# Keeping split weights in DRAM after the first of four blocks, in a one-core transformer layer in fp32

## What is computed

```python
x = x + attn(cond(x, cond_weights, itok_B_0_15), Wq, Wk, Wv, Wo, q_norm_w, k_norm_w)
x = x + ffn(cond2(x, weight, bias, lora_a, lora_b, scaling, itok_B_1_7), W_base, b_base, enc0, ...)

# cond:  einsum('bct,bcd->bdt', x, weights[condition])
# attn:  q = x @ Wq.T (32 heads), k = x @ Wk.T, v = x @ Wv.T (8 heads), rmsnorm(q), rmsnorm(k),
#        softmax(q k^T / sqrt(128) + alibi, causal) v, then @ Wo.T
# cond2: x @ weight.T + bias + a low-rank term chosen for each sequence
# ffn:   x @ W_base.T + b_base + 0.5 * (an inverse Fourier transform of masked low-rank terms)
```

## Time and profile before

| | us |
|---|---|
| median of 3 runs | 2668.3 |
| lowest and highest | 2659.5 and 2669.61 |
| the profiled execution | 2667.39 |
| its span, first to last instruction | 2665.6 |

### The profile page before, as it was taken

How to read it: one execution, slowest core, us unless ns; L and a number is a source line. 1 busy time by engine, 2 the same in 40 slices (tenths; PEclk the granted TensorE clock), 3 DMA queues, 4 the chain that set the end, 5 groups by cost and what they waited for, 6 DMA issues and landing times.

```text
span 2665.6 us, 32724 instructions
## 1 busy us (share of the span) xinstructions
PE 2441.8 (92%) x11676; PEld 1995.5 (75%) x11676; DVE 1811.7 (68%) x2830; ACT 1249.5 (47%) x2881; POOL 431.5 (16%) x336
## 2 busy tenths in 40 slices
PE   7989989898899999999899999898989989899988
PEld 5867767676678777777778777777768878787867
DVE  5557768676845767676854777767774686867682
ACT  3235545353524545454633555555542554545450
POOL 0101212120211111111121121112130121212021
PEclk8989999999999999999999999999999999999999
DMA  5261433525343141414234141423243132323241
GB/s 206 103 253 64 167 141 135 190 91 194 128 142 111 64 142 65 141 64 142 95 122 149 64 143 64 133 73 126 73 143 135 64 119 87 119 88 111 95 150 48
DMA packets 88436, 316.13 MB, mean 119 GB/s; under 512 B 12716, under 2 KB 13228, under 8 KB 87124
## 3 DMA queue, kind: packets, MB, share of 16 engines
q1 hardware_dynamic: 70292, 247.14, 27.4%
q10 hardware_dynamic: 10944, 37.54, 3.8%
q0 software_dynamic: 7040, 29.36, 3.0%
HBM read 282.54 MB, written 31.46 MB: 118 GB/s over the span
## 4 chain that ended last, share of the span: by engine, by line
PE 61%; DVE 21%; DMA 6%; issue 6%; ACT 4%; POOL 1%; ACTq 0%; POOLq 0%; DVEq 0%
PE main L926 50%; DVE ring L1367 9%; DMA raw<-in_wo 4%; PE qt_bank L1075 2%; ACT ring L1121 2%; DMA sums<-in_wo 2%; DVE qn L1501 2%; PE s_bank L1091 2%; DVE qn L1494 2%; DVE pt_lo L1557 1%; DVE score L1370 1%; PE pv_bank L1110 1%; PE s_bank L1092 1%; POOL rstd L1666 1%; DVE lefts L1367 1%
## 5 line engine op out<-in xcount | busy, mean ns | idle before, releaser
L926 PE MATMUL main<-ring,act_hi 128*128 128x512 f32 x3584 | 1155.8, 404 | 0.0
L926 PEld LDWEIGHTS main<-ring,act_hi 128*128 128x128 f32 x3584 | 646.4, 190 | 112.8
L926 PE MATMUL main<-ring,act_lo 128*128 128x512 f32 x1792 | 705.4, 394 | 0.0
L926 PE MATMUL main<-ring,lefts 128*128 128x512 f32 x2688 | 655.7, 403 | 45.4 <-ACT main L1121 24.6
L1367 DVE TENSOR_TENSOR ring<-raw,ring 128x1024 fp32r<-128x1024 f32 x448 | 607.1, 1364 | 89.5 <-ACT ring L1121 88.2
L1121 ACT ACTIVATE ring<-raw 128x1024 fp32r<-128x1024 f32 x448 | 473.4, 1061 | 400.7 <-PE main L926 274.4
L926 PEld LDWEIGHTS main<-ring,lefts 128*128 128x128 f32 x2688 | 517.8, 195 | 162.2 <-ACT main L1121 29.7
L1666 POOL TENSOR_TENSOR rstd<-mean,half 128x4 f32<-128x4 f32 (+1 forms) x192 | 179.7, 936 | 1606.8 <-DVE mean L1477 1606.8
L926 PEld LDWEIGHTS main<-ring,act_lo 128*128 128x128 f32 x1792 | 339.1, 189 | 75.4
L1075 PE MATMUL qt_bank<-ident,qn 128*128 128x128 f32 x640 | 108.5, 285 | 119.4 <-DVE qn L1501 62.8
L1243 ACT ACTIVATE sq<-main 128x128 f32<-128x128 f32 x640 | 168.8, 277 | 76.7 <-PE main L926 74.4
(11 more groups left out here) (142 smaller groups left out, 2595.3 us busy)
## 6 DMA issues: line engine op xcount, KB each, us to landing
raw<-in_wq SPq DMA_DIRECT2D x128, 512.0 KB, 4.1
raw<-t_scratch SPq DMA_DIRECT2D x128, 512.0 KB, 3.3
raw<-in_wo SPq DMA_DIRECT2D x96, 512.0 KB, 3.3
raw<-in_wkv SPq DMA_DIRECT2D x64, 512.0 KB, 4.2
sums<-in_wo ACTq DMA_DIRECT2D x32, 512.0 KB, 6.3
t_scratch<-sums ACTq DMA_DIRECT2D x32, 512.0 KB, 4.4
raw<-f_scratch SPq DMA_DIRECT2D x32, 512.0 KB, 4.0
acc<-in_x POOLq DMA_DIRECT2D x16, 512.0 KB, 3.6
```

The source lines that it names most:

```text
L926: mm = eng.matmul(bank, a, b, start=start and n == 0 and m == 0, stop=stop and n == len(terms) - 1 and m == 2, skip_group_check=further)
```

## The change

In block 0 each chunk is loaded and split as before, and then the two halves of 84 of the 112 chunks (all of `kv`, `q` and `f`, and the even ones of `o`; `is_kept`) are stored together, 1 MB, from `ring` to `w_scratch` in DRAM (`w_store`, issued by SP). In blocks 1 to 3 these chunks are loaded from there straight into their slot of `ring` (`ring{i}`, SP, 1 MB) with no work on ACT or DVE; the 28 odd chunks of `o` are loaded raw and split as before, and their raw load is issued just ahead of the 1 MB load of the chunk before. There are 4 raw buffers in place of 3 (the query gain takes the bytes of `score` to make room). Split chunks are planned at least 1.8 quarters apart in place of 1. `t_load` to `t_store` are spread out, with 5.5 quarters from load to `t1` in place of 3.5. `s1`, `s4` and `v7_add` go from POOL to DVE, at later places.

```diff
-RAWS = 3
+RAWS = 4
...
-LEFT_AT = (dict(s3=-9, s2=-3, s1=0.5, s4=2.5, op=(-8, -6, -2, 4.4, 8.4, 12.4, 16.4)),
+LEFT_AT = (dict(s3=-9, s2=-3, s1=2.6, s4=6.6, op=(-8, -6, -2, 4.4, 8.4, 12.4, 16.4)),
...
+def is_kept(kind, c):
+
+    return kind != "o" or c % 2 == 0
...
             if n >= SLOTS:
-                last = max(free[n - SLOTS] + AT["w_hi"], last + 1)
-            out.append(last)
+                if self.is_halves(n):
+                    before = max(free[n - SLOTS], before)
+                else:
+                    before = last = max(free[n - SLOTS] + AT["w_hi"], last + 1.8, before)
+            out.append(before)
         return out
+
+    def is_halves(self, n):
+
+        u, c = self.chunks[n]
+        kind, blk, number = self.units[u]
+        return blk > 0 and is_kept(kind, c)
...
-        self.load(n, ("w_lo", (n,)))
+        if self.is_halves(n):
+            if n + 1 < len(self.chunks) and not self.is_halves(n + 1):
+                self.load(n + 1, ("w_lo", (n + 1,)))
+            self.add(f"ring{n % SLOTS}", n)
+            return
+        if blk == 0:
+            self.load(n, ("w_lo", (n,)))
         self.add("w_hi", n)
+
+        def rest():
+            self.add("w_lo", n)
+            if blk == 0 and is_kept(kind, c):
+                self.add(f"w_store{n % SLOTS}", n)
...
-        for pair in range(KV_HEADS // 2):
-            self.right_factors(pair)
+
+        for at, pair in ((0, 0), (28, 1)):
+            self.right_factors(pair, at, 14)
+        for pair in (2, 3):
+            self.right_factors(pair, QUARTERS * (self.first_step["o", 0, pair - 2] + len(OPS)), 19)
...
         self.add("v7_out", k, tp)
-        self.add("v7_add", k, tp)
+        self.later(1.5, lambda: self.add("v7_add", k, tp))
...
+                elif stage.startswith("w_store"):
+                    n, = key
+                    w.wait_ge("w_lo", n)
+                    eng.dma_start(w_scratch[n], f32(ring[:, n % SLOTS, :, :])).then_inc(done[stage], 16)
+                elif stage.startswith("ring"):
+                    n, = key
+                    made = n % per_block
+                    w.wait_ge(f"w_store{made % SLOTS}", made)
+                    slot_free(w, n)
+                    eng.dma_start(f32(ring[:, n % SLOTS, :, :]), w_scratch[made]).then_inc(done[stage], 16)
```

More of the change, by code:

```diff
@@ L368, in prepare @@
             self.gather(blk)
-        self.load(n, ("w_lo", (n,)))
+        if self.is_halves(n):
[5 more added lines that the diff above has]
+            self.load(n, ("w_lo", (n,)))
         self.add("w_hi", n)
+        def rest():
+            self.add("w_lo", n)
+            if blk == 0 and is_kept(kind, c):
+                self.add(f"w_store{n % SLOTS}", n)
         if both:
-            self.add("w_lo", n)
+            rest()
         else:
-            self.later(AT["w_lo"] - AT["w_hi"], lambda: self.add("w_lo", n))
+            self.later(AT["w_lo"] - AT["w_hi"], rest)
     def blocks(self):
@@ L611 @@
 DMA_STAGES = ("coefs", "masks", "mixidx", "const", "mixw_load", "first", "raw", "x", "out", "f_store",
-              "t_load", "t_store", "fx_load", "fx_store")
+              "t_load", "t_store", "fx_load", "fx_store", "ring", "w_store")
 def is_dma(stage):
@@ L758, in setup_part, with slot_free @@
             return setup[:, UNIT_CHUNKS * slot + c, part, :]
+        per_block = len(order.chunks) // BLOCKS
+        w_scratch = nc.dram_tensor("w_scratch", [per_block, P, 2, CHUNK], F32).ap()
+        def slot_free(w, n):
+            before = n - SLOTS
+            if before < 0:
+                w.wait_ge("weff_mm", KT, n // UNIT_CHUNKS, n % UNIT_CHUNKS)
+                return
+            u, c = order.chunks[before]
+            unit = order.units[u]
+            if unit[0] == "o":
+                w.wait_ge("mm", order.first_step[unit] + c // 2, 2 + c % 2)
+            else:
+                w.wait_ge("mm", order.first_step[unit] + TILES - 1, c)
+            if unit[1] == 0 and is_kept(unit[0], c):
+                w.wait_ge(f"w_store{before % SLOTS}", before)
         def ring_part(n, part):
@@ L946, in weights_here @@
             def weights_here(n):
-                w.wait_ge("w_hi", n)
-                w.wait_ge("w_lo", n)
+                if order.is_halves(n):
+                    w.wait_ge(f"ring{n % SLOTS}", n)
+                else:
+                    w.wait_ge("w_hi", n)
+                    w.wait_ge("w_lo", n)
             for stage, key in order.stages:
@@ L1303, in _ @@
                     elif blk == 0:
+                        if pair > 0:
+                            w.wait_ge("mm", order.left_before[k], 3)
                         for i in range(4):
-                            w.wait_ge(f"t_store{i}", pair, 1)
+                            w.wait_ge(f"t_store{i}", min(pair + 1, 3), 1)
                     else:
```

81 lines of the change are left out of this document (36 added, 45 removed).

## The result

The changed kernel takes 2947.8 us (median of 4 runs, 2947.2 to 2953.5) against 2669.0 before: ratio 1.106, 95% interval 1.103 to 1.109. The profiled execution's span is 2945.5 us. I had forecast 2800, with a range up to 2930: the sign was right, the loss about twice the one forecast (+279 in place of +133).

The account below looks back on a forecast made before the run. PE was taken as the bound, with only its gaps and the slow stretches behind them to win. Block 0 +238 and blocks 1 to 3 -105 gave +133 on 2667.4, so 2800 us; 8-in-10 range 2650 to 2930.

Parts of the forecast that it names:

- the slow clock: Block 0: PE at its lower clock behind a dozen new waits of 3 to 5 us, +20 us, at most 30.
- Blocks 1 to 3, -105: Later blocks: 252 splits and POOL's sums go, so PE's waits and slow clock shrink; saves 105 us, bounds 80 and 120.
- Block 0, +238: First block: raw loads lose their lead, only one ahead where three were; 238 us longer, bounds +85 and +338.
- L: Block 0: time for a raw load right behind a 1 MB store to land, 5.1 us, bounds 3.3 and 6.1.
- The round, 7.9: Block 0, chunks in a row: store issue, load, upper half, lower half and hand-overs take 7.9 us per chunk (6.1 to 8.9).
- Unit ends: Block 0, eight ends other than around `o`: 26.3 us where 16.5 before; 9.8 us each, 78 in all (35 to 102).
- Around `o`: Block 0, four `o` units: 100.1 us from first upper half to query transposes, before 64.0; 36 each, 144 (65 to 188).
- End of the setup: Before block 0's first key transposes: five rounds put them at 184.8 instead of 167.86, costing 17 us (8 to 22).
- A store costs the next load nothing: Rival, chance 0.16: block 0 loads still land in 3.3 us, block 0 loses only 85, later blocks gain 120; 2632 us.
- Transfers as the bound in later blocks: Rival, chance 0.13: 1 MB loads land late, 57 us over later blocks, and block 0 is +314; 2933 us.
- Half of the store out of the way: Rival, chance 0.20: block 0 loads land in 4.2 us, rounds 7.0 and 8.5, +164 in block 0; 2726 us.
- Less saved: Rival, chance 0.07: other DVE work is as late in blocks 1 to 3, which save 60 in place of 105; 2845 us.

## Why the prediction was right and wrong, point by point

**The step that failed.** The mechanism of block 0 held. What failed is the size of one term of its sum, the slow clock: +20, at most +30, where PE's busy time rose by 104. A second term was too small as well, the length and number of the rounds, which left idle time at +279 where I had +218. The measured +279 is still inside what my upper bound leaves for idle time (338 less 30); the clock's 104 is what carried the time over the range.

**The bound.** Right. What changed the time was PE's gaps, and the slow matmuls behind them.

**Blocks 1 to 3, -105.** Right in sum: -99 by the stretches, -105 from block to block. The agreement to the microsecond is luck: my terms add up to 116, and I went on from the 120 that I had called "at most"; the waits for `lefts` were not in it; and with the sums left on POOL the same halves bring 74. It was wrong in what it rests on. I gave nearly all to splits that go away, and to POOL's operation 1.6 of the 2.8 us that I took off one wait for the gain. I had its row, a gain of 2.12 us that ends behind POOL's sum, and took it for one place; the group mean of the earlier trace rows, 1364 ns against 1.22 us undisturbed, said that there were more of them, 44 among the lower halves alone. Either half of the change alone gets some 70 of the 104 us. The query scaling went with the splits, as I had said; the gain went mostly with the sums. The new wait of 3 us for ring loads was 1.3, though they landed in 6.2 us and not in 5.8; the 4 us a block that I held back for dense places did not show as a wait for loads.

**Block 0, +238.** The mechanism is what I described: SP's queue at `w_lo`, the load behind the store, ACT's head of queue, 581 us of waits for `raw`. The size was +383, beyond my upper bound of +338. Below, unit ends, `o` units and the setup divide it by place, and the slow clock by kind: two ways to count the same microseconds, not to be added.

- *L.* Assumed 5.1; measured 5.7 for a lone load behind a store (page, `in_wq`), within the bounds. The single store in front costs 2.4 us over the 3.3 of the earlier trace rows; behind the load in place of in front of it, it costs 0.9 (4.2).
- *The round, 7.9.* 8.4 at best, 9.4 on average in the row of four that is shown. What is over comes from the term that I had as a sentence and not as a number: ACT stands at `w_hi`, the query's lower half on DVE gets late by it, and the next `w_lo` stands behind that.
- *Unit ends.* I gave 26.3 us from the first upper half to the scores; here it is 31.3 (264.30 to 295.62, the first row below), and at the same unit end before it was 16.8. At the unit end of the earlier trace rows, 16.5 us before, it is 33.4. From the first `o` row's start to the second's it is 231.9 us (364.14 to 596.07) in place of 146.7, of which the `o` row takes 53 (next point), so two unit ends take 32: 16 us each, not 9.8. With the two next points taken off the 386 us of block 0, 145 are left for all of them, not 78.
- *Around `o`.* 100.1 forecast from the first upper half to the query transposes, 117.1 measured, by the last two rows below; before 64.0. The four cost 53, 53, 46 and, where the two `f` units follow, 70 us: 222, not the 147 of my `o` and `f` terms.
- *End of the setup.* 17 forecast; the key transposes start at 186.63, 18.8 us later than before. Right.
- *Slow clock.* The step that failed most. I added 20 us; PE's busy time rose by 104. The measured times of the two places above hold their share of it, which my rounds, made of loads and halves alone, did not: in place of the dozen new waits that I counted there are 58 gaps where there were 20, and many are longer than 5 us. So of the 145 us missed in block 0, 84 are slow matmuls and 61 idle time (279 against 218).

In the changed kernel: PE's first score behind the row of four; then ACT's first and last upper half of the first `o` row, and PE's transposes behind it.

```profile
295.62 0.44 PE L1150 MATMUL s_bank<-k_t,qt_hi 128*128 128x128 f32 x1 [3.24 <-ACT qt_hi L1180]
```

```profile
364.14 1.06 ACT L1180 ACTIVATE ring<-raw 128x1024 fp32r<-128x1024 f32 x1 [0.53 <-issue]
...
476.94 1.06 ACT L1180 ACTIVATE ring<-raw 128x1024 fp32r<-128x1024 f32 x1 [11.50 <-DMA raw<-in_wq]
```

```profile
481.20 1.12 PE L1134 MATMUL qt_bank<-ident,qn 128*128 128x128 f32 x4 [15.77 <-DVE qn L1547]
```

**The rivals.** *A store costs the next load nothing*: refuted, 5.7 and not 3.3. Moreover its price was wrong: with the load ahead of the store `in_wq` loads land in 4.2 us, the L for which I had worked out 2726, and that kernel took 2801. The sign does not turn where I had put it by a straight line: a line through these two kernels (4.2 and 2801, 5.7 and 2948) meets the time before at an L of 2.9, less than a lone load takes. That is an estimate; no run tests it. *Transfers as the bound in later blocks*: refuted, 1.3 us of waits, and the run with all chunks kept. My 340 GB/s, worked out from a busy share, is no ceiling: in block 0 of that run the DMAs moved 386 GB/s between 321.2 and 385.5 us, which is also more than the limit that I had set beside it. *Half of the store out of the way*: refuted by the 5.7, and by the 2801 for its price. *Less saved* (60): refuted, 99 to 105.

**The range.** Its top was the forecast's upper end; the bounds took L, which was known to 1 us, at its worst, and left the count of gaps, which was not known, nearly fixed. The 30 us that I allowed at most for the slow clock was the bound that broke, by 74.

## What to carry to other kernels

A DMA that waits for a producer must not stand in an in-order queue ahead of loads that others wait for: issue the loads first, as far as buffers go, or give it a queue of its own. Here the same transfers cost +386 us or -17 in block 0, by their order alone. Where a chain of waits makes many gaps of a few microseconds, price the slow matmuls behind them with the gaps; here they were a third or more on top. And look for operations of VectorE whose mean is above their shortest: they may be blocked by GpSimd. Whether they are shows in their ends, which then follow GpSimd's by the same time for each shape (1.08 us for the lower halves, 0.28 for the gains), and moving work *onto* the busier engine may be what frees it.

## What the hardware showed that I had not expected

- A VectorE addition with two SBUF inputs that starts beside a GpSimd sum waits for the rest of it: up to 3.43 us in place of 1.22. An operation of VectorE with one input in PSUM does not (0.42 us in both cases). Taking 64 such sums onto VectorE lowered VectorE's busy time by 35 us and the kernel's by 93.
- Behind a 1024 KB store in the same queue a 512 KB load lands in 5.7 us, and in 4.2 with the store behind it; alone it takes 3.3. The store in front adds about half of its own 4.8 us, although it goes the other way.
- With three loads ahead, loads of block 0 land later (median 7.2 us against 5.9) at 288 GB/s in place of 179, and ACT waits less for them, 75.5 us in place of 581. With all chunks stored they land later still (median 10.8) at 312 GB/s.
